# Storing the transposed rows of one stage for the tiles of the next, in a one-core attention and mixture-of-experts kernel on Trainium2

## The reference

```python
x = x + tanh(g_xattn) * mlstm(layernorm(x), ctx, ctx)        # 16 heads, gates from q, k, v
x = x + tanh(g_ffn) * moe(layernorm(x))
# moe(f), f of 4096 x 1024:
probs = softmax(f @ router_w.T); topk_w, topk_idx = top_k(probs, 2)   # 16 experts
shared = silu(f @ shared_gate_w) * (f @ shared_up_w) @ shared_down_w  # 1024 wide
routed = sum over the row's 2 experts: w * (silu(f @ gate_w[e]) * (f @ up_w[e])) @ down_w[e]   # 512 wide
output = shared + routed
```

## Time and profile before

| | |
|---|---|
| median of 3 runs (lowest to highest) | 3125.04 us (3122.43 to 3129.82) |
| the profiled execution's own time | 3112.9 us |
| its span, first to last instruction | 3111.3 us |
| TensorE busy | 2968.8 us (95%) |
| VectorE, ScalarE, GpSimd busy | 1626.6 us (52%), 1012.4 us (33%), 595.4 us (19%) |
| mean granted TensorE clock | 0.983 of full speed |
| bytes moved by DMA | 441.92 MB, 142 GB/s |

### The profile page before, as it was taken

How to read it: one execution, slowest core, us unless ns; L and a number is a source line. 1 busy time by engine, 2 the same in 40 slices (tenths; PEclk the granted TensorE clock), 3 DMA queues, 4 the chain that set the end, 5 groups by cost and what they waited for, 6 DMA issues and landing times.

```text
span 3111.3 us, 50365 instructions
## 1 busy us (share of the span) xinstructions
PE 2968.8 (95%) x17262; PEld 2453.0 (79%) x17263; DVE 1626.6 (52%) x3104; ACT 1012.4 (33%) x1916; POOL 595.4 (19%) x572
## 2 busy tenths in 40 slices
PE   4799999999999988999999999999999999999999
PEld 3687878787877876888888888888888888888887
DVE  4787878787788864342243324323333344444444
ACT  4444434344444422232233333322333331111111
POOL 1234333333334321000000000000000001111111
PEclk9799999999999998999999999999999999999999
DMA  6454455454554444133433333333334324444444
GB/s 192 143 166 149 143 136 172 137 150 136 168 147 143 142 151 149 62 139 138 142 135 142 136 140 142 135 142 142 135 142 142 135 81 150 147 141 159 144 138 152
DMA packets 205735, 441.92 MB, mean 142 GB/s; under 512 B 86784, under 2 KB 87680, under 8 KB 205056
## 3 DMA queue, kind: packets, MB, share of 16 engines
q1 hardware_dynamic: 110544, 333.62, 32.1%
q0 software_dynamic: 24400, 72.96, 7.2%
q10 hardware_dynamic: 70656, 33.56, 4.1%
HBM read 350.72 MB, written 107.18 MB: 147 GB/s over the span
## 4 chain that ended last, share of the span: by engine, by line
PE 59%; DVE 1%; ACT 1%; ACTq 0%; issue 0%; DVEq 0%
PE p_g_b L1568 19%; PE p_up_b L1568 19%; PE p_y_b L1556 17%; PE p_x_b L1536 3%; PE p_h_b L1543 1%; DVE w_lo L1420 1%; ACT w_hi L1363 1%; ACTq L1217 0%; ACTq L1202 0%; DVE x L1476 0%; DVE sg_b L1448 0%; DVE x L1467 0%; ACT th_b L1405 0%; DVE y_b L1478 0%; ACTq L1359 0%
## 5 line engine op out<-in xcount | busy, mean ns | idle before, releaser
L1568 PE MATMUL p_g_b<-w_hi,xt_hi_b 128*128 128x512 f32 x840 | 342.2, 407 | 16.3 <-DVE w_lo L1420 13.0
L1436 DVE TENSOR_TENSOR ht_lo_b<-p_h_b,ht_hi_b 128x512 fp32r<-128x512 f32 x105 | 72.5, 691 | 542.7 <-ACT ht_hi_b L1375 542.7
L1556 PE MATMUL p_y_b<-w_hi,ht_hi_b 128*128 128x512 f32 x840 | 339.9, 405 | 1.9 <-DVE ht_lo_b L1436 1.9
L1568 PE MATMUL p_up_b<-w_hi,xt_lo_b 128*128 128x512 f32 x840 | 331.6, 395 | 0.0
L1448 DVE SCALAR_TENSOR_TENSOR sg_b<-th_b,p_g_b 128x512 f32<-128x512 f32 x105 | 72.3, 688 | 494.6 <-ACT th_b L1405 494.6
L1568 PE MATMUL p_up_b<-w_lo,xt_hi_b 128*128 128x512 f32 x840 | 330.4, 393 | 0.0
L1568 PE MATMUL p_g_b<-w_hi,xt_lo_b 128*128 128x512 f32 x840 | 329.9, 393 | 0.0
L1556 PE MATMUL p_y_b<-w_lo,ht_hi_b 128*128 128x512 f32 x840 | 329.5, 392 | 0.0
L1568 PE MATMUL p_up_b<-w_hi,xt_hi_b 128*128 128x512 f32 x840 | 327.8, 390 | 0.0
L1568 PE MATMUL p_g_b<-w_lo,xt_hi_b 128*128 128x512 f32 x840 | 327.3, 390 | 0.0
L1556 PE MATMUL p_y_b<-w_hi,ht_lo_b 128*128 128x512 f32 x840 | 326.5, 389 | 0.0
(11 more groups left out here) (221 smaller groups left out, 5700.4 us busy)
## 6 DMA issues: line engine op xcount, KB each, us to landing
mid_y<-y_b SPq DMA_DIRECT2D x73, 512.0 KB, 3.2
stage<-mid_g_row SPq DMA_DIRECT2D x64, 512.0 KB, 5.1
stage<-in_eg SPq DMA_DIRECT2D x16, 2048.0 KB, 9.1
stage<-in_eu SPq DMA_DIRECT2D x16, 2048.0 KB, 15.3
stage<-in_ed SPq DMA_DIRECT2D x16, 2048.0 KB, 19.5
mid_y<-in_x SPq DMA_DIRECT2D x34, 512.0 KB, 8.9
stage<-in_x SPq DMA_DIRECT2D x32, 512.0 KB
stage<-in_ctx_t ACTq DMA_DIRECT2D x32, 512.0 KB, 7.9
```

Source lines behind the costliest of these rows:

```text
L1436: nc.vector.tensor_tensor(ht_lo[:, :, :], p_h[:, :, :], ht_hi[:, :, :].bitcast(f32), ALU.subtract).then_inc(ht_rdy, 1)
L1556: last = nc.tensor.matmul(p_y[n][:, :], a[:, k, :], b[:, GUP + k, w], start=(k == 0 and m == 0), stop=(k == FE // P - 1 and m == 2))
L1568: mm = nc.tensor.matmul(out[:, :], a[:, k, :], w[:, k, o:o + FE], start=(k == 0 and m == 0), stop=(k == KD - 1 and m == 2))
```

## The change

The merged stage stores both parts of each transposed tile, 1 MB, to a new DRAM tensor `mid_xt` (new part M of the table, on SP, right behind part N). ScalarE's copy into `xt` waits until the store of the tile before has landed. In the routed stage the shared tiles 1 to 31 load that from DRAM into one of two buffers `xts`, on GpSimd's queue, and have no transposes, no `x_high` and no `x_low`; SP's `load_x` goes. Tile 0 of the shared tiles is transposed as before. The loop over the shared tiles holds two bodies per pass, one for each buffer. A table of 128 x 1024 that was a buffer of its own (`hot`) uses `x1`.

```diff
-                "F1", "Y3", "A5", "J1", "Y4", "N1", "W3", "B3", "A6", "L1", "N2", "T1", "W4", "S1", "Q1", "G1", "W5",
+                "F1", "Y3", "A5", "J1", "Y4", "N1", "W3", "B3", "A6", "L1", "N2", "M1", "T1", "W4", "S1", "Q1", "G1", "W5",
...
+            def stage_m(part, b, j):
+                c = b * CPB + j
+                sp.wait_ge(xl_sb, 2 * c + 2)
+                sp.dma_start(t["xt"][c], xt[:, :, :, :].bitcast(f32)).then_inc(xt_out, 16)
...
             sp.wait_ge(xn_out, 16 * NCH)
+            sp.wait_ge(xt_out, 16 * NCH)
...
                 ge(act, gu_ps, c)
+                ge(act, xt_out, 16 * c)
                 act.wait_ge(xn_ps, 2 * c + n + 1)
...
-        xt_hi, xt_lo = sb("xt_hi", [P, KD, P], f32r), sb("xt_lo", [P, KD, P], f32r)
+        xts = [sb(f"xt{n}", [P, 2, KD, P], f32r) for n in range(2)]
+        xt_hi, xt_lo = xts[0][:, 0, :, :], xts[0][:, 1, :, :]
...
-            body(n + 1, n, NE, 1, False, "shared", False)
-            with eng.Fori(2, NCH - 1) as c:
-                body(n + c, n + (c - 1), NE, c, False, "shared", False)
-            body(n + (NCH - 1), n + (NCH - 2), NE, NCH - 1, False, "shared", True)
+            body(n + 1, n, NE, 1, False, "shared", False, 1)
+            with eng.Fori(1, NCH // 2 - 1) as m:
+                body(n + 2 * m, n + (2 * m - 1), NE, 2 * m, False, "shared", False, 0)
+                body(n + (2 * m + 1), n + 2 * m, NE, 2 * m + 1, False, "shared", False, 1)
+            for left in (2, 1):
+                c = NCH - left
+                body(n + c, n + (c - 1), NE, c, False, "shared", True, c % 2)
...
-            def load_x(c):
-                sp.wait_ge(xt_ps, before + c)
-                sp.dma_start(xg[:, :], xn_rows[c]).then_inc(xs_in, 16)
...
                 if prev == "shared":
                     gather(c - 1, c)
+                if isinstance(c, int) and c == 0:
+                    pool.dma_start(xts[1][:, :, :, :], t["xt"][1]).then_inc(xs_in[1], 16)
+                if c is not None and not last:
+                    load_xt(i, c + 2, slot or 0)
+
+            def load_xt(i, c, slot):
+
+                ge_apart(pool, past, (gu_ps, i + 1))
+                pool.dma_start(xts[slot][:, :, :, :], t["xt"][c]).then_inc(xs_in[slot], 16)
...
-                if not last:
+                if c is None:
                     x_high(i + 1)
...
-                if not last:
+                if c is None:
                     x_low(i + 1)
...
+                high, low = (xt_hi, xt_lo) if slot is None else (xts[slot][:, 0, :, :], xts[slot][:, 1, :, :])
+                if slot is not None:
+                    pe.wait_ge(xs_in[slot], 8 * (c + slot))
...
-                if not last:
+                if c is None:
                     turn_x(i + 1, c)
```

More of the change, by code:

```diff
@@ L169, in mix_block @@
         gu0_hi, gu0_split = keep["gu0_hi"], keep["gu0_split"]
-        xn_out = sem("xn_out")
+        xn_out, xt_out = sem("xn_out"), sem("xt_out")
         fill_in = sem("fill_in")
@@ L215, in mix_block @@
         OFFSET = {"X": 3, "L": 2, "Q": 2, "T": 2, "A": 1, "S": 1, "F": 1, "B": 0, "W": 0, "C": -1, "R": -1,
-                  "D": -2, "E": -2, "N": -2, "G": -2, "P": 0, "K": -3, "U": -3, "H": -3, "Y": -3, "J": -3,
+                  "D": -2, "M": -2, "E": -2, "N": -2, "G": -2, "P": 0, "K": -3, "U": -3, "H": -3, "Y": -3, "J": -3,
                   "V": -1, "Z": -2, "O": -3}
@@ L450, in _ @@
             schedule(sp, None, {"P": stage_p, "X": stage_x, "R": stage_r, "W": stage_w, "A": stage_a, "D": stage_d,
-                                "F": stage_f, "E": stage_e, "J": stage_j, "V": stage_v, "Z": stage_z}, sp.Fori)
+                                "F": stage_f, "E": stage_e, "J": stage_j, "M": stage_m, "V": stage_v, "Z": stage_z}, sp.Fori)
             sp.wait_ge(xn_out, 16 * NCH)
+            sp.wait_ge(xt_out, 16 * NCH)
             sp.wait_ge(fill_in, 16 * SPARE)
@@ L1175, in ffn_block @@
         first_row = sb("first_row", [P, NE])
-        hot = sb("hot", [P, 2 * NCH, NE])
+        hot = keep["x1"][:, 0, :].rearrange("p (n e) -> p n e", e=NE)
         slot_f, slot_i = sb("slot_f", [P, 2 * NCH]), sb("slot_i", [P, 2 * NCH], i32)
@@ L1180, in ffn_block @@
         wg_in, wu_in, wd_in = keep["w0_in"]
-        xs_in = sem("xs_in")
+        xs_in = [sem(f"xs_in{n}") for n in range(2)]
         x_in, idx_in, mid_out = keep["row0_in"], keep["idx0_in"], keep["mid_out"]
@@ L1271, in _ @@
             load_base(0)
-            load_x(2)
-            with sp.Fori(1, NCH - 4) as c:
-                load_x(c + 2)
+            with sp.Fori(1, NCH - 1) as c:
                 load_base(c)
                 store_joined(c)
[L1277 to L1286, removed]
+            ge(sp, gu_split, GUP * (NE + 1))
+            sp.dma_start(last_base, base_rows[NCH - 1]).then_inc(last_base_in, 16)
+            store_joined(NCH - 1)
             for n in range(2):
@@ L1316, in _, with body @@
             list_parts = t["lists"].rearrange("(n p) w -> n p w", p=P)
-            def body(i, q, e, c, first, prev, last):
+            def body(i, q, e, c, first, prev, last, slot=None):
                 if first:
@@ L1322, in body @@
                     return
-                if c is None or isinstance(c, int) and c < 2:
+                if c is None or isinstance(c, int) and c < 1:
                     rows_of(i, e, c, first)
@@ L1525, in _ @@
         def _(pe):
-            trio = ((xt_hi, w_hi), (xt_lo, w_hi), (xt_hi, w_lo))
             def turn_x(i, c):
[L1531 to L1534, removed]
+                pe.wait_ge(x_in, 16 * i + 16)
                 for k in range(KD):
@@ L1558, in down, with body @@
                     last.then_inc(y_ps, 1)
-            def body(i, q, e, c, first, prev, last):
+            def body(i, q, e, c, first, prev, last, slot=None):
                 ge(pe, h_rdy, i)
+                high, low = (xt_hi, xt_lo) if slot is None else (xts[slot][:, 0, :, :], xts[slot][:, 1, :, :])
+                if slot is not None:
+                    pe.wait_ge(xs_in[slot], 8 * (c + slot))
                 for k in range(KD):
-                    if k % 4 == 0:
+                    if slot is None and k % 4 == 0:
                         pe.wait_ge(xt_rdy, 2 * i + (k // 4 + 1))
                     pe.wait_ge(gu_split, GUP * e + (k + 1))
-                    for m, (a, w) in enumerate(trio):
+                    for m, (a, w) in enumerate(((high, w_hi), (low, w_hi), (high, w_lo))):
                         for out, o in ((p_g, 0), (p_up, FE)):
@@ L1591, in build @@
                   "eidx": [P, 2 * NCH], "rank": [P, 2 * NCH], "wts": [P, 2 * NCH]}
+        t["xt"] = nc.dram_tensor("mid_xt", (NCH, P, 2, KD, P), f32, kind="Internal").ap()
         t["s_row"] = nc.dram_tensor("mid_s_row", (NH, P), f32, kind="Internal").ap()
```

## The result

The changed kernel takes **3104.82 us** (median of 4 runs, 3102.77 to 3106.33), the kernel before 3127.43 us on the same chip (4 runs, 3122.43 to 3132.3): a ratio of 0.9927, 95% interval 0.9909 to 0.9946. It is faster, by 22.6 us; predicted were 3098.0 us and 27.0 us less.

The account below looks back on a forecast made before the run. PE's instruction stream was taken to bound the shared tiles; 31 tiles x 0.87 us of transposes = 27.0 us off the 3125.04 us median gave 3098.0 us, with load and store costing nothing; range 3081 to 3116.

Parts of the forecast that it names:

- What bounds the kernel: Shared tiles of the routed stage: PE is busy for all 520 us, so only its instruction stream's length counts.
- The term of 0.87 us a tile: Shared tiles 1 to 31: by instruction starts, removing eight PE transposes saves 0.87 us each tile, 27.0 us in all.
- rival E: Shared tiles: each transpose holds PE for its recorded 0.273 us, so 67.7 us go, giving 3057; chance 1%.
- The load: Shared tiles: GpSimd's 1 MB load per tile lands in about 5 us of 22.4 allowed and costs nothing.
- The store: Merged stage: SP's 1 MB store per tile is hidden, costing the residual's x load 3 to 5 us of 8.7 spare.
- Rival A: Merged stage: the store makes the residual's x land 2.0 us late, net + 29 us, 3154; chance 5%.
- rival B: Shared tiles: the two-body loop is fetched at every jump, 3.4 us a pass, net + 20 us, 3145; chance 3%.
- The sum: Whole kernel: 27.0 us off the profiled 3112.9 gives 3085.9; off the median 3125.04 gives 3098.0 us.
- Rival C: Merged stage: loses 10 to 20 us through late x or more bad jumps, 3108 to 3118; chance 13%.
- The bounds of -17 and +13 us: Merged stage, first turns of batches: all five stalled turns mild gives 17 us less, all five bad 13 us more.
- a sign of being wrong: Merged stage as a whole moving by more than 17 us, or a shared tile giving back less than 0.8 us.
- The jump itself: Merged loop's jump back: VectorE stalls up to 5.2 us, 16.8 us in all, read as instruction fetch; PE's clock then falls.

## Why the prediction was right, and where it was not

The mechanism and the sign were right, and the time lies in the range, 6.8 us above the forecast. Of those, 2.4 us are the kernel before, whose median was 3127.43 in the comparison and not 3125.04, and 4.4 us are gain that the first comparison did not show.

**What bounds the kernel.** Right. PE is busy for the whole shared stretch, 520 us before and 500 after, and waits for nothing there.

**The term of 0.87 us a tile.** Right. 17.79 became 16.92 us, and putting the eight transposes back made it 17.80. The reading by starts holds, and rival E, 3057 us by their recorded 0.273 us, is out: it would have made the tile 17.79 - 8 x 0.273 = 15.6 us. The figure of about 275 ns, which stands beside a bf16 transpose (the ones here are f32), in the Trainium skill, "TensorE: Matmul & The Clock Gate", "Part 4: PE-mode transpose", agrees with the recorded length and not with what a transpose costs in this stream, 0.87 / 8 = 0.11 us.

**The load.** Right: estimated at about 5 us, landed in 5.3, with 22.4 us allowed. The gathers behind it lost the forecast 0.8 us of cover in one tile (issued at 3026.14, used at 3036.49 us, 10.4 later) and 1.7 in the tile before it (3010.13 to 3019.57, 9.4). One of them was late, as VectorE's group of the second weighted row shows for 2580 to 3080 us (busy us, mean ns, idle before and its releasers):

```profile
L1474 DVE SCALAR_TENSOR_TENSOR x<-x,wts 128x1024 f32<-128x1024 f32 x30 | 38.5, 1285 | 5.9 <-DVE x L1470 4.5 <-DMA x<-mid_y,slot_now_b 1.3
```

In the 30 tiles 1.3 us in all, in one tile, went to waiting for a gather; VectorE's 4.9 us before `ht_lo` in each tile cover that.

**The store.** Right that it is free, but two of its terms came out otherwise. What it costs the load of x behind it was taken as 3 to 5 us; it is 0.7 (that load lands in 4.0 us in the median, 3.3 before). And it was to fall into an empty stretch and take 3.2 us if alone; it took 9.4 in the median. SP issues it 2.75 us behind the store of z, while that is still moving. The empty 8 us of the earlier trace rows begin only 7.7 us behind the store of z, so they were no measure for it. In the turn shown, the DMA engines are full until 660 us and two thirds busy in the 4 us after that (columns as above):

```profile
652.00:656.00 4.00, 4.00 (x54) 3.47 (x53) 3.76 (x6) 2.51 (x10) 3.42 (x3) 1.00 1.04 339
656.00:660.00 4.00, 4.00 (x19) 3.26 (x18) 3.45 (x18) 3.40 (x11) 1.28 (x1) 1.00 1.02 409
660.00:664.00 4.00, 4.00 (x23) 3.37 (x22) 3.93 (x5) 1.55 (x2) 0.00 (x0) 1.00 0.67 227
```

The load of x is issued at 660.38, so only its first 2 us or so meet the last of the store (652.97 + 9.4 = 662.4, by the median). Its spare time is 8.7 us as predicted, but by luck: the time from issue to use and the landing both grew by 0.7. Rival A decides from 0.84 us of delay per tile on PE; twice the bytes did not bring that.

**The loop of two bodies** (rival B). From tile 1 on, every shared tile lasted 16.92 or 16.93 us, also at the jumps. Out.

**The sum, and the 4.4 us.** The first comparison gave 0.9927 where 27.0 / 3125 asks for 0.9914, which lies inside its interval. Rival C, a loss in the merged stage, describes the first profile: 15.6 us in 27 turns. It does not describe the change. With the store alone the ratio is 0.9998, the changed kernel timed again twice gives 0.9903 both times, and its profiles there have 935.3 and 936.6 us in those 27 turns against 935.9 before. So the shortfall is most likely scatter of a stage that the change does not touch on PE.

That scatter was priced too low. The bounds of -17 and +13 us were built from the turns behind a stall alone, and the first profile is 15.6 us longer in the 27 turns and 19.6 up to the 31st tile, more than the 17 us that the prediction named as a sign of being wrong. By that pair alone it would have failed its own test; the two later profiles, 1034.3 and 1035.7 us to the 31st tile against 1036.4, do not repeat it. Only part of the loss sits where the prediction put the uncertainty: the five turns behind a stall took 35.9, 40.3, 40.2, 37.3 and 34.1 us before and 39.8, 35.4, 37.6, 38.6 and 42.2 in the first profile after, 5.8 us more in all, out of 15.6. Another 2.8 us stand in the first turn of batch 1 (35.0 us for 32.2). The rest is spread over ordinary turns, which the prediction expected to keep their length: the third turn of each batch from 1 to 6 lasts 33.9 us in the kernel before and in all ten experiments, with the store or without it, and 34.1 to 34.6 in that one profile. Its cause is open.

**The jump itself.** That a long stall there costs a long turn and a fallen clock is shown. That the stall is instruction fetch is argued, not shown: the instruction queue moves where it occurs and hardly elsewhere, as the next section shows, but no run made the loop shorter, so this was not tried.

## What to carry to other kernels

Where PE is busy for a whole stage and waits for nothing, the gain of removing instructions from it is their start-to-start time, not their recorded length; here that was 0.11 against 0.273 us, and the forecast held to 0.01 us per tile. A store placed in front of a load on a queue cost nothing here, because what uses the load had 8.7 us of slack; but judge a landing by the traffic that is still moving at the moment of issue (9.4 us here, where 1 MB alone at 326 GB/s would take 3.2). When the gain is under 1%, cut the profiles at the boundary of the changed stage: the part with the change was steady within 5 us here, while the stage before it moved by up to 30 us from one execution to another and could hide or fake the whole effect in a single pair.

## What the runs showed of the hardware that was not expected

The wait at the jump back of the long loop differs from pass to pass and from execution to execution. In the changed kernel's three profiles the five waits of VectorE behind it last between 1.8 and 6.1 us (5.05, 1.79, 2.10, 4.17, 6.09 in the first), the longest in any kernel was 7.3 us (store twice), and the turn mostly goes with it: 34.1 us behind a wait of 1.98, 40.2 behind 5.06, 42.2 behind 6.09 (but 37.3 behind 2.17). In the longest of these turns more than two fifths of the loss is not PE's standing but its lower clock afterwards: 4.4 of 10.1 us.

The two instruction queues of the changed kernel from 200 to 1030 us, the merged loop, and from 1300 to 2140 us, the routed tiles (packets, MB, share):

```profile
q8 instruction: 59, 0.97, 0.5%
q14 instruction: 37, 0.30, 0.2%
...
q8 instruction: 2, 0.03, 0.0%
q14 instruction: 2, 0.02, 0.0%
```

So the instruction queues move again and again in the merged loop and hardly in the routed one. Whether the DMA traffic sets the length of the stalls is not shown. With the store doubled, at 208 GB/s in the 27 turns for 179 in the changed kernel beside it, they sum to 21.6 us for 14.6, but the store alone at 177 GB/s gave 21.7, and the median time of the doubled store was only 0.7 us longer.
